# Routing of a mixture of experts in two groups of batches, the first one inside the attention loop's last iterations

## The reference

```python
# x [32, 100, 256], ctx [32, 361, 256]; E = 8 experts, 256 -> 512 -> 256
x = x + layernorm(attention(q=layernorm(x), kv=ctx, 16 heads) + layernorm(x))   # 32 batches
t = layernorm(x)
z = layernorm(t) * ln_g + ln_b
probs = softmax(z @ rW + rb)                    # over the 8 experts
topv, topi = top_k(probs, 2)
w = topv / max(sum(topv), 1e-8)                 # gates of the two chosen experts
x = x + t + sum over the 2 chosen e of w_e * (gelu(z @ W1[e] + b1[e]) @ W2[e] + b2[e])
```

## Time and profile before

| | us |
|---|---|
| median of 3 runs | 1063.49 (1058.77 to 1065.8) |
| profiled execution | 1064.32 |
| its span in the trace | 1062.5 |
| last logits end (L852) | 762.4 |
| first expert matmul starts (L1052) | 819.9 |

### The profile page before, as it was taken

One profiled execution on the slowest core, in us unless ns is written; L12 is line 12 of the kernel. 1 busy time (PEld: TensorE's weight loads), 2 busy tenths in 40 slices (PEclk: granted clock), 3 DMA queues, 4 the chain that ended last, 5 costly groups with the idle time before them and its releaser, 6 DMA issues. The chain is left out here.

```text
span 1062.5 us, 26290 instructions
## 1 busy us (share of the span) xinstructions
PE 780.8 (73%) x7982; PEld 593.0 (56%) x7983; DVE 716.0 (67%) x1903; ACT 509.4 (48%) x1286; POOL 622.6 (59%) x612
## 2 busy tenths in 40 slices
PE   3358677778887878788778887866113999999990
PEld 2135455555555555555555555544003999999980
DVE  2169777787878788778878878883285555555550
...
GB/s 155 151 124 134 83 95 103 120 131 93 106 129 116 93 104 143 109 89 114 139 100 97 116 134 102 119 86 68 156 274 30 51 66 65 66 66 67 66 55 126
DMA packets 158047, 112.68 MB, mean 106 GB/s; under 512 B 69485, under 2 KB 151749, under 8 KB 157477
## 3 DMA queue, kind: packets, MB, share of 16 engines
...
...
## 5 line engine op out<-in xcount | busy, mean ns | idle before, releaser
L793 DVE TENSOR_REDUCE negmax<-s_row 100x1 f32<-100x361 f32 x512 | 255.0, 524 | 107.3 <-PE s_row L492 104.9
L650 ACT ACTIVATE p_t<-s_t 128x400 f32<-128x400 f32 x384 | 182.8, 505 | 237.0 <-PE s_t L511 229.3
L492 PE MATMUL s_row<-k_stack,q_stack 125*128 125x361 bf16 x512 | 148.9, 346 | 102.9 <-DMA k_stack<-k_part 53.4
L523 PE MATMUL zt<-p_t,v_aug 128*32 128x100 f32 (+1 forms) x3072 | 95.3, 258 | 62.0 <-DVE p_t L810 45.0
L511 PE MATMUL s_t<-q_stack,k_stack 128*128 128x100 bf16 x1536 | 126.2, 214 | 3.1 <-DMA q_stack<-m_part 2.2
L523 PEld LDWEIGHTS zt<-p_t,v_aug 128*32 128x32 f32 (+1 forms) x3072 | 66.5, 112 | 109.9 <-DVE p_t L810 92.9
L478 PE MATMUL pj<-wv_s,ct 128*128 128x256 f32 x384 | 120.2, 443 | 0.0
L492 PEld LDWEIGHTS s_row<-k_stack,q_stack 125*128 125x128 bf16 x512 | 43.0, 103 | 135.8 <-issue 88.0
L1052 PE MATMUL p_h<-zgt,w_k 128*128 128x128 f32 x912 | 113.0, 278 | 2.0 <-DVE w_k L1275 2.0
L511 PEld LDWEIGHTS s_t<-q_stack,k_stack 128*128 128x128 bf16 x1536 | 94.8, 102 | 30.3 <-issue 12.0
L1052 PEld LDWEIGHTS p_h<-zgt,w_k 128*128 128x128 f32 x912 | 107.9, 194 | 2.9 <-DVE w_k L1275 2.4
...
## 6 DMA issues: line engine op xcount, KB each, us to landing
k_stack<-k_part SPq DMA_DIRECT2D x192, 192.0 KB, 4.6
q_stack<-q_part SPq DMA_DIRECT2D x192, 64.0 KB, 2.0
...
```

Of the source, the lines that this page charges most:

```text
L492: nc.tensor.matmul(s_row[h % 2][:, 0:KEYS], q_stack[0:MROW, b.slot, h, :], k_stack[0:MROW, b.slot, h, 0:KEYS], start=True, stop=True).then ...
L523: last = nc.tensor.matmul(zt[32 * j:32 * j + 32, quad * Q:quad * Q + Q], v_aug[0:n, b.slot, kt * H + 4 * quad + j, :], p_t[0:n, quad % 2, ...
L650: nc.scalar.activation(p_t[:, quad % 2, kt, :], s_t[g % 2][:, 0:4 * Q], ACT.Exp).then_inc(exp_done, 1)
L793: v.tensor_reduce(negmax[:, h:h + 1], s_row[h % 2][0:Q, 0:KEYS], AXIS.X, ALU.max, negate=True).then_inc(max_done, 1)
```

## The change

The tiles of the routing that were in the second block now lie, as slices, in tiles of the attention block that are dead by then: `w2_s` in `k_stack`, `b2_s` in `p_t`, the constants in `k_rest`, the routing's work tiles in `ct` and `v_raw`, the one-hot lanes of the first group in `k_part`. The routing is split in two groups of batches. Batches 0 to 23 are routed by instructions placed in slots of i = 31 to 33 (logits of batch 23 are there since i = 26); batches 24 to 31 in the second block, with their prefix sums started from the first group's last row. Lane and tile are taken from the place within the expert's own list, so that only `tile_of` gets the expert's first tile added afterwards (`moved`, `shift`). The product with the batch number moves from POOL to DVE; `tile_hot` and `picked` have four buffers. `te_i` and the first two `weights` come while PE still inverts. `w1_s` is loaded by ACT's DMA queue at i = 27 to 30, two experts each, `w2_s` by ACT at i = 31 to 33 (two, three and three experts), `b2_s` at i = 34, and `odd_d` is zeroed by eight DMAs of 400 KB in SP's queue, one at the end of the first iteration of each turn of the loop. The core of the diff (`route(dve, ins)` is the old `step`):

```diff
+EARLY = 24
+GROUPS = [slice(0, EARLY), slice(EARLY, B)]
...
+        ct = sb(es, "ct", [128, 3, 2, KPAD])
+        k_part = sb(es, "k_part", [128, 3, 3, 2, KPAD], BF16)
+        k_rest = sb(es, "k_rest", [128, 2, KEYS])
+        k_stack = sb(es, "k_stack", [128, 3, H, KPAD], BF16)
+        v_raw = sb(es, "v_raw", [128, KT * H, DH])
+        p_t = sb(es, "p_t", [128, 2, KT, 4 * Q])
+        w2_s = k_stack[:].rearrange("p s h k -> p (s h k)")[:, 0:2 * E * 4 * D].bitcast(FP32).rearrange("p (e c f) -> p e c f", e=E, c=4)
+        b2_s = p_t[:].rearrange("p a t k -> p (a t k)")[:, 0:E * D].rearrange("p (e f) -> p e f", e=E)
+        lane_early = k_part[:].rearrange("p a s t k -> p (a s t k)")[0:Q, 0:2 * EARLY * 128].rearrange("q (c b w) -> q c b w", c=2, b=EARLY)
...
+        def ask_exponentials(dve, group):
+            v, part = nc.vector, GROUPS[group]
+            route(dve, v.tensor_reduce(col[0][:, part], logits[:, part], AXIS.X, ALU.max))
+            v.tensor_tensor(big1[:, part], logits[:, part], over_e(col[0][:, part]), ALU.subtract).then_inc(exp_asked, 1)
+        def route_exponentials(act, group):
+            part = GROUPS[group]
+            act.wait_ge(exp_asked, group + 1)
+            nc.scalar.activation(pr[:, part], big1[:, part], ACT.Exp).then_inc(exp_ready, 1)
+        def probabilities(dve, group):
+            v, part = nc.vector, GROUPS[group]
+            dve.wait_ge(exp_ready, group + 1)
+            route(dve, v.tensor_reduce(col[0][:, part], pr[:, part], AXIS.X, ALU.add))
+            route(dve, v.reciprocal(col[1][:, part], col[0][:, part]))
+            route(dve, v.tensor_tensor(pr[:, part], pr[:, part], over_e(col[1][:, part]), ALU.mult))
+        def choose(dve, group, c):
+            v, part = nc.vector, GROUPS[group]
+            revb = rev.unsqueeze(1).broadcast_to([Q, part.stop - part.start, E])
+            if c == 0:
+                dve.wait_ge(cst_loaded, 32)
+            src = (pr, big0)[c]
+            route(dve, v.tensor_reduce(wt[:, c, part], src[:, part], AXIS.X, ALU.max))
+            route(dve, v.tensor_tensor(big1[:, part], src[:, part], over_e(wt[:, c, part]), ALU.is_equal))
+            route(dve, v.tensor_tensor(big1[:, part], big1[:, part], revb, ALU.mult))
+            route(dve, v.tensor_reduce(col[c][:, part], big1[:, part], AXIS.X, ALU.max))
+            route(dve, v.tensor_tensor(choice[:, c, part], revb, over_e(col[c][:, part]), ALU.is_equal))
+            if c == 0:
+                route(dve, v.scalar_tensor_tensor(big0[:, part], choice[:, 0, part], -2.0, pr[:, part], ALU.mult, ALU.add))
+            else:
+                v.tensor_tensor(big0[:, part], choice[:, 0, part], choice[:, 1, part], ALU.add).then_inc(picks_ready, 1)
+        def gates(dve, group):
+            v, part = nc.vector, GROUPS[group]
+            route(dve, v.tensor_tensor(col[0][:, part], wt[:, 0, part], wt[:, 1, part], ALU.add))
...
+            for c in range(2):
+                v.tensor_tensor(wq2[:, part, c], wt[:, c, part], col[1][:, part], ALU.mult).then_inc(gates_ready, 1)
+        def store_gates(sp, group):
+            part = GROUPS[group]
+            sp.wait_ge(gates_ready, 2 * group + 2)
+            sp.dma_start(zf_d[part, :, D:ROW].rearrange("b q c -> q b c"), wq2[:, part]).then_inc(gates_stored, 16)
+        def sum_choices(pe, bank, group):
...
+            nc.tensor.matmul(bank[0:Q, 0:n], sums[:, 0:Q], picks, start=True, stop=True)
+            nc.tensor.matmul(bank[0:Q, 256:256 + n], sums[:, Q:2 * Q], picks, start=True, stop=True).then_inc(sums_done, 1)
...
+        def local_places(dve, bank, group, before):
+            v, part = nc.vector, GROUPS[group]
+            route(dve, v.tensor_tensor(base[:, part], before, sum_rows(bank, 0, group), ALU.add))
+            for c in range(2):
+                route(dve, v.tensor_tensor(big1[:, part], base[:, part], choice[:, c, part], ALU.mult))
+                route(dve, v.tensor_reduce(loc[:, c, part], big1[:, part], AXIS.X, ALU.add))
+            route(dve, v.tensor_copy(loc_i[:, 0, :, part], loc[:, :, part]))
+            route(dve, v.tensor_scalar(loc_i[:, 1, :, part], loc_i[:, 0, :, part], 127, None, ALU.bitwise_and))
+            route(dve, v.tensor_copy(lane[:, :, part], loc_i[:, 1, :, part]))
+            route(dve, v.tensor_scalar(loc_i[:, 1, :, part], loc_i[:, 0, :, part], 7, None, ALU.logical_shift_right))
+            route(dve, v.tensor_copy(tile_of[:, :, part], loc_i[:, 1, :, part]))
...
-                    if isinstance(turn, int) and i >= 36 - E:
-                        e = i - (36 - E)
-                        sp.dma_start(w1_s[:, :, e, :], w1[e].rearrange("(c p) f -> p c f", p=128)).then_inc(w1_loaded, 16)
+                    if isinstance(turn, int) and i == 30:
+                        sp.wait_ge(k_low_ready, B)
+                        sp.dma_start(cst, route_c).then_inc(cst_loaded, 16)
+                        sp.dma_start(sums, sum_c).then_inc(cst_loaded, 16)
+                    if isinstance(turn, int) and i == 33:
+                        store_gates(sp, 0)
+                    if not isinstance(turn, int) and i == 0:
+                        zeroed = odd_d[bass.ds(turn * 4 - 4, 4)].rearrange("b q d -> (b q d)").rearrange("(p r n) -> p r n", p=16, n=400)
+                        sp.dma_start(zeroed, pad_rows[0:16].bitcast(FP32)[:, 0:400].unsqueeze(1).broadcast_to([16, 16, 400])).then_inc(odd_zeroed, 16)
...
+                        if isinstance(turn, int) and (i, s) == (32, 5):
+                            pe.wait_ge(v01_biased, B)
+                            sum_choices(pe, pj[1], 0)
...
+                    if isinstance(turn, int) and 27 <= i < 31:
+                        for e in (2 * (i - 27), 2 * (i - 27) + 1):
+                            act.dma_start(w1_s[:, :, e, :], w1[e].rearrange("(c p) f -> p c f", p=128)).then_inc(w1_loaded, 16)
+                    if isinstance(turn, int) and 31 <= i < 34:
+                        last = i - 2
+                        act.wait_ge(s_t_done, NG * (last + 1))
+                        for e in range(E)[3 * (last % 3):3 * (last % 3) + 3]:
+                            act.dma_start(w2_s[:, e], w2[e].rearrange("(c p) f -> p c f", p=128)).then_inc(w2_loaded, 16)
+                    if isinstance(turn, int) and i == 34:
+                        act.wait_ge(pv_done, G * B)
+                        act.dma_start(b2_s, b2.unsqueeze(0).broadcast_to([128, E, D])).then_inc(w2_loaded, 16)
...
+                        if isinstance(turn, int) and (i, s) == (31, 8):
+                            route_exponentials(act, 0)
...
+                def early_prefix():
+                    dve.wait_ge(sums_done, 1)
+                    for k in range(2):
+                        v.memset(cum[k][:, 0:16, :], 0.0).then_inc(route_step, 1)
+                        routed[0] += 1
+                    route(dve, v.tensor_copy(cum[0][:, 16:, :], sum_rows(pj[1], 256, 0)))
+                    at = 0
+                    for k in (1, 2, 4, 8, 16):
+                        route(dve, v.tensor_tensor(cum[1 - at][:, 16:, :], cum[at][:, 16:, :], cum[at][:, 16 - k:16 + EARLY - k, :], ALU.add))
+                        at = 1 - at
+                def early_lanes(m):
+                    c, half_part = m // 2, slice(m % 2 * EARLY // 2, (m % 2 + 1) * EARLY // 2)
...
+                    v.tensor_tensor(lane_early[:, c, half_part], lanes.unsqueeze(1).broadcast_to([Q, EARLY // 2, 128]),
+                                    lane[:, c, half_part].unsqueeze(2).broadcast_to([Q, EARLY // 2, 128]), ALU.is_equal).then_inc(lanes_early, 1)
...
+                        if isinstance(turn, int) and (i, s) == (31, 5):
+                            dve.wait_ge(logits_ready, EARLY)
+                            ask_exponentials(dve, 0)
+                        if isinstance(turn, int) and (i, s) == (31, 9):
+                            probabilities(dve, 0)
+                        if isinstance(turn, int) and (i, s) in ((32, 1), (32, 3)):
+                            choose(dve, 0, s // 2)
+                        if isinstance(turn, int) and (i, s) == (32, 5):
+                            gates(dve, 0)
+                        if isinstance(turn, int) and (i, s) == (32, 9):
+                            early_prefix()
+                        if isinstance(turn, int) and (i, s) == (33, 1):
+                            local_places(dve, pj[1], 0, cum[1][:, 15:15 + EARLY, :])
+                        if isinstance(turn, int) and (i, s) in ((33, 4), (33, 6), (33, 9), (33, 11)):
+                            early_lanes((4, 6, 9, 11).index(s))
...
-                sp.dma_start(cst[:], route_c).then_inc(cst_loaded, 16)
-                sp.dma_start(sums[:], sum_c).then_inc(cst_loaded, 16)
-                for e in range(E):
-                    sp.dma_start(w2_s[:, :, e, :], w2[e].rearrange("(c p) f -> p c f", p=128)).then_inc(w2_loaded, 16)
                 sp.dma_start(b1_s[:], b1).then_inc(w2_loaded, 16)
```

(64 more changed lines are left out.)

187 lines of the change are left out of this document (75 added, 112 removed).

## The result

The changed kernel takes 1069.61 us (median of 17 runs, 1063.77 to 1083.39), the kernel before 1064.29 (median of 17, now more runs than the three shown ahead). One of the 17 took 1909.98 us, and it and one run of the changed kernel (1083.39) were in a slow state and are left out of the ratio. The ratio is 1.0051, 95% interval 1.0026 to 1.0076: the change makes the kernel slower by half a per cent. The forecast was 1056 us. The profiled execution took 1071.13 us with a span of 1069.3.

The account below looks back on a forecast made before the run. PE alone bounds the expert stage; the routing's 57.5 us are a nearly serial chain, and attention's end waits on another. 1064.3 - 21.2 (routing) + 12.1 (tail) + 1.2 (loop) = 1056.4, so 1056 us; 8-in-10 range 1046 to 1068.

Parts of the forecast that it names:

- What left the 57.5 us: Routing, last logits to first expert matmul: shorter steps leave 36.3 us of 57.5, a gain of 21.2 (18 to 23).
- In-order pieces of the tail: Before the last logits: pieces in DVE's and PE's own order delay what queues behind them, 2.3 + 0.5 + 1.3 + 0 + 5.0 us.
- `probabilities` and the first `choose`: Attention's last iterations on DVE: three steps ahead of a guard, 0.5 us (0 to 1.0); first choose in a hole.
- the second `choose`: At (32, 3) on DVE, ahead of batch 31's last guard: six steps of 0.38, 2.3 us.
- `local_places`: With early_prefix in DVE's 6.14 us wait before batch 31's statistics: nothing, or 0.5 us if the cover shrinks.
- `sum_choices`: With the gates at (32, 5), matmuls on PE ahead of a transpose: 1.3 us (0.5 to 1.6).
- the lanes: Four early_lanes instructions on DVE in i = 33, delaying the statistics' aggregation and POOL: 5.0 us (1.7 to 6.8).
- W2 beside `zscr`: Tail: W2's loads hold back zscr's DRAM round trips, 1.2, 1.3 and 0.5 us, less 0.5: 2.5 (0 to 8).
- the credit of 0.5 for the W1 load: Tail: SP's w1_s load no longer stands ahead of the small DMAs PE waited for; 0.5 us deducted.
- ACT's issues: Attention's last iterations: ACT spends some 0.5 us per DMA issue, mostly in idle time; cost 0.5 us (0 to 2).
- The loop: Attention loop: zeroing DMAs ahead of q_stack's and W1 loads beside k_stack's cost 1.2 us (0 to 14).
- the zeroing holds up the loop: Rival, attention loop: narrow-source zeroing delays q_stack DMAs; at 2.5 us for each of eight, 1076 us; chance 0.11.

Follow-up runs that it names:

- e12: Kernel before with only W1's loads moved, two by two on the ScalarE queue at i = 27 to 30; ratio to the kernel before 0.9971.
- e3: Changed kernel with both the zeroing and the W2 and b2 loads back in the second block; ratio to the kernel before 0.9948.
- e4: Kernel before with only the zeroing moved into the attention loop, eight 400 KB DMAs from 16 partitions; ratio to the kernel before 1.0068.
- e5: Kernel before with the zeroing in the attention loop, same bytes and place, but read from 128 partitions instead of 16; ratio to the kernel before 1.0010.
- e6: Changed kernel with the zeroing back in the second block and W2's loads issued between the zscr trips; ratio to the kernel before 0.9880.

## Why the prediction was wrong

**What left the 57.5 us**: right. 36.3 us were forecast, 35.3 measured. Late steps 0.26 us (0.25 taken), products 1.11, tile tables and W1 copies ahead of the indices 4.2 as summed, 2.4 of them behind PE's last matmul. One reading was off: the 5.13 us of `sums` were not a busy queue in general but W1's load right ahead of it (e12); the sum doesn't change.

**In-order pieces of the tail**: near in sum, 10.1 us for the 2.3 + 0.5 + 1.3 + 0 + 5.0 = 9.1 of the forecast, and that by luck, since its errors cancel. With W2 out of the way (e3) the tail is 9.2 us longer, although the transposed scores of batch 31 start 0.8 us earlier than before. From there `probabilities` and the first `choose` cost 1.4 (0.5 forecast, 1.0 its bound, and the first `choose` at nothing), the second `choose` 2.6, `local_places` 0.8 in a hole that I had at nothing, `sum_choices` nothing where 1.3 were taken (0.5 its lower bound), the lanes 5.3 for 5.0. The list's upper bounds add up to 22.2, not 21.

**W2 beside `zscr`**: the mechanism right, the size wrong, and this is the first failed step. I took 1.2 + 1.3 + 0.5 = 3.0 us, 2.5 with the credit of 0.5 for the W1 load; it was 7.3 (60.8 less 53.5). The credit can't be told from scatter: e3 has the transposed scores 0.8 us earlier, but e4 and e5, with the W1 load in its old place, have them as early within 0.3. By the marks of the kernel after and of e3 the 7.3 are 2.4, 3.2 and 1.8 for batches 29, 30 and 31. The trips themselves lost 2.9, 4.6 and 2.3 us, the second beyond its own bound of 3. I had sized the load by 1 us for 512 KB from SP's issue times, and an issue is not a transfer: three loads ran for 6.6 us, 2.2 each. And I had assumed that only half of a load would meet the trip, when those of batches 29 and 30 leave at the same moment as `zscr` and it shares the engines with them to their end. Batch 31's left 3.5 us ahead.

**ACT's issues**: forecast 0.5, nothing could be found (e6's three megabytes were free).

**The loop**: the second failed step, and the larger. I took 1.2 us out of 0 to 14, on two premises: a zeroing lasts 0.8 us by the rate of W2's loads, and the small `q_stack` DMAs behind it are not waited for in the loop. Its rate was 102 GB/s, not the 500 that this assumed, because of its 16 partitions; its packets ran for 4.2 us, and PE waited for the small DMAs in the loop, four times and 6.3 us in the kernel after, seven times and 11.3 in e4, never in the kernel before. The eight cost about 7 us (e4). The rival "the zeroing holds up the loop" was this mechanism, named with its cause; it had 0.11, and its price of 2.5 us apiece was too high: 7.2 us are 0.9 for each.

Measured terms in the forecast's sum, 1064.3 - 22.2 + 16.6 + 7.2, give 1066; the measured 1069.6 is 3.7 above. The interval of e4's 7.2 us (3 to 11) covers that, so whether it is chance or a further cost in the loop is open; W1's loads could be 1 to 3 us of it. The loop's length in single profiles is too scattered to decide it: of the 13.8 us between the profiled loops, about 10 go with 34 us more at the lower clock by the estimate above, and this profile's granted clock, 0.870, is the lowest of the changed kernel's 17 runs (0.870 to 0.887).
